# Entity batch times weights on one core: x and W packed side by side in memory, larger and smaller transfers, one reduce for the three parts

## What is computed

```python
def reference(r_entity_idxs, L0_rec_W):       # (1024, 12500) of 0.0 and 1.0, (128, 12500), float32
    entities = jnp.einsum('be,le->bl', entity_idxs, W)
    s = jnp.sum(entity_idxs, axis=1)
    s_safe = jnp.where(s != 0, s, 1.0)
    scale = jnp.where(s != 0, 1.0 / s_safe, 1.0)
    return entities * scale[:, None]          # (1024, 128)
```

## Time and profile before

| | |
|---|---|
| time, median of 3 runs | 155.78 us |
| span of the profiled execution (first to last instruction) | 154.0 us |
| TensorE busy | 133.4 us, 87% |
| VectorE, ScalarE busy | 90.6 us, 80.3 us |
| DMA | 58.20 MB, mean 378 GB/s |

### The profile page before, as it was taken

How to read it: one execution, slowest core, us unless ns; L and a number is a source line. 1 busy time by engine, 2 the same in 40 slices (tenths; PEclk the granted TensorE clock), 3 DMA queues, 4 the chain that set the end, 5 groups by cost and what they waited for, 6 DMA issues and landing times.

```text
span 154.0 us, 2291 instructions
## 1 busy us (share of the span) xinstructions
PE 133.4 (87%) x785; PEld 76.6 (50%) x785; DVE 90.6 (59%) x93; ACT 80.3 (52%) x103; POOL 0.5 (0%) x8
## 2 busy tenths in 40 slices
PE   0198999989989989989989989989989989999900
PEld 0043656545545545546545545545545545545500
DVE  0443975838538528628727826835845746648950
ACT  3462755464474464465456447437527527556720
POOL 1000000000000000000000000000000000000000
PEclk9999999999999999999999999999999999999985
DMA  5999999999999999999999999999999999999220
GB/s 165 320 417 423 412 429 421 412 422 419 421 421 417 422 422 417 426 419 419 421 421 419 421 419 418 424 417 419 426 417 413 432 417 406 349 348 346 90 61 4
DMA packets 13866, 58.20 MB, mean 378 GB/s; under 512 B 1148, under 2 KB 6480, under 8 KB 8228
## 3 DMA queue, kind: packets, MB, share of 16 engines
q1 hardware_dynamic: 13860, 58.13, 94.2%
HBM read 57.60 MB, written 0.52 MB: 377 GB/s over the span
## 4 chain that ended last, share of the span: by engine, by line
DMA 61%; PE 12%; issue 7%; DVE 6%; ACT 5%; SPq 4%; ACTq 0%; DVEq 0%
DMA x_sb<-x_t 61%; PE acc L414 12%; DVE w_parts L308 4%; ACT w_parts L230 3%; ACT act_out L236 1%; SPq L152 1%; SPq L156 1%; DVE w_rest L301 1%; ACT w_parts L224 1%; SPq L170 1%; SPq L190 0%; DVE y_sum L354 0%; SPq L161 0%; SPq L166 0%; DVE low_max L313 0%
## 5 line engine op out<-in xcount | busy, mean ns | idle before, releaser
L414 PE MATMUL acc<-w_parts,x_sb 128*128 128x385 bf16 (+1 forms) x784 | 133.2, 331 | 13.1 <-DVE w_parts L308 7.8
L414 PEld LDWEIGHTS acc<-w_parts,x_sb 128*128 128x128 bf16 (+1 forms) x784 | 76.6, 99 | 69.4 <-issue 16.1
L236 ACT ACTIVATE act_out<-x_sb 128x2048 bf16<-128x2048 uint16 (+4 forms) x31 | 48.0, 1549 | 42.5 <-DMA x_sb<-x_t 42.5
L313 DVE TENSOR_REDUCE low_max<-x_sb 128x2048 uint16 (+4 forms) x31 | 56.5, 1831 | 1.6 <-DMA x_sb<-x_t 1.6
L301 DVE TENSOR_TENSOR w_rest<-w_raw,w_parts 128x1024 f32<-128x1024 f32 (+2 forms) x14 | 15.2, 1091 | 37.8 <-ACT w_parts L224 37.8
L308 DVE TENSOR_TENSOR w_parts<-w_rest,w_parts 128x1024 bf16<-128x1024 f32 (+2 forms) x14 | 15.2, 1093 | 16.0 <-ACT w_parts L230 16.0
L224 ACT ACTIVATE w_parts<-w_raw 128x1024 bf16<-128x1024 bf16 (+2 forms) x14 | 13.3, 955 | 18.4 <-PE acc L414 12.7
L230 ACT ACTIVATE w_parts<-w_rest 128x1024 bf16<-128x1024 bf16 (+2 forms) x14 | 13.1, 943 | 1.9 <-DVE w_rest L301 1.9
L236 ACT ACTIVATION_READ_ACCUMULATOR act_out<-x_sb (+2 forms) x31 | 5.8, 187 | 0.0
L354 DVE TENSOR_TENSOR y_sum<-acc,y_sum 128x128 f32<-128x128 f32 x16 | 4.4, 280 | 0.8 <-ACT y_sum L269 0.7
L269 ACT ACTIVATE y_sum<-acc 128x128 f32<-128x128 f32 x8 | 2.2, 275 | 3.0 <-PE acc L414 2.9
(11 more groups left out here) (7 smaller groups left out, 0.8 us busy)
## 6 DMA issues: line engine op xcount, KB each, us to landing
x_sb<-x_t SPq DMA_DIRECT2D x46, 1024.0 KB, 16.5
w_raw<-w_t SPq DMA_DIRECT2D x12, 512.0 KB, 12.9
x_sb<-x_t SPq DMA_DIRECT2D x3, 512.0 KB, 9.4
x_sb<-x_t SPq DMA_DIRECT2D x4, 256.0 KB, 7.8
out<-y SPq DMA_DIRECT2D x4, 128.0 KB, 2.2
x_sb<-x_t SPq DMA_DIRECT2D x1, 336.0 KB
w_raw<-w_t SPq DMA_DIRECT2D x1, 64.0 KB
w_raw<-w_t SPq DMA_DIRECT2D x1, 42.0 KB
```

Source lines behind the costliest of these rows:

```text
L236: nc.scalar.activation(act_out[0:rows, buf, 0:tiles * n].rearrange("p (j b) -> p j b", j=tiles), low, ACT.Copy, accum_out=low_max[0:rows, ...
L313: nc.vector.tensor_reduce(low_max[0:rows, bass.ds(col, 1)], low, AX.XY, ALU.max).then_inc(dve_checked, count)
L414: return nc.tensor.matmul(acc[:, b, 0:N], x_top[0:rows, s, j, b * P:(b + 1) * P], w_parts[0:rows, s, j, :], start=first, stop=last)
```

## The change

x and W are laid out by the host in the order in which they are loaded. `main` holds 20 units; in a unit each of 128 partitions has one row of 18432 B: x of 4 tiles (4 x 4096 B) and W of 4 tiles (4 x 512 B) of the unit that follows. `ends` holds the pieces of both ends: a short one (84 rows, x and W of one tile), two ramp pieces (x of 1 and 2 tiles; W of 3 and 4), six taper pieces (x of 2, 2, 2, 2, 1, 1 tiles; the first two with W of 4 and 6 tiles), and the x of the last 4 tiles in six final pieces by users: three of 256 users x 4 tiles, one of 128 x 4, two of 128 x 2. 4 slots of one unit stand in place of 2 of a block; ramp, taper and final pieces have buffers of their own. SP waits, for a unit, until its slot's 32 matmuls and both checks are done.

`rest` and `lo` now read the upper halves of the words themselves and no longer wait for ScalarE's `hi` and `mid`. The three parts of a bank are added by one `tensor_reduce` from PSUM on VectorE, ScalarE does all the scaling, and the banks go out in pairs but for the last two, each alone. Users are dealt to banks in another order (`reshape(P, B // P, E)`), so that a pair of banks is written in rows of 1024 B. The general path works tile by tile in a loop; TensorE's part of it is 48 matmuls long in place of 272.

```diff
-T = 8
-CHUNK = 2
-CHUNKS = T // CHUNK
-SLOTS = 2
...
-PIECE = 2
+T = 4
+SLOTS = 4
+MAIN = 20
+RAMP_X = (1, 2)
+RAMP_W = (3, T)
+TAPER_X = (2, 2, 2, 2, 1, 1)
+TAPER_W = (T, 6, 0, 0, 0, 0)
+LAST = 4
+FINAL = ((0, 2, 0, 4), (2, 4, 0, 4), (4, 6, 0, 4), (6, 7, 0, 4), (7, 8, 0, 2), (7, 8, 2, 4))
+TILES = sum(RAMP_X) + MAIN * T + sum(TAPER_X)
...
+def pieces(short, B, L):
+    shapes = [(short, B + L)]
+    shapes += [(P, x * B + w * L) for x, w in zip(RAMP_X, RAMP_W)]
+    shapes += [(P, x * B + w * L) for x, w in zip(TAPER_X, TAPER_W)]
+    shapes += [(P, (j1 - j0) * (b1 - b0) * P) for b0, b1, j0, j1 in FINAL]
+    at, table = 0, []
+    for rows, cols in shapes:
+        table.append((at, rows, cols))
+        at += rows * cols
+    return table, at
...
-    LOADS = [(q, 0, T) for q in range(PIECES - 2)]
-    LOADS += [(PIECES - 2, j, j + T // 2) for j in range(0, T, T // 2)]
-    LOADS += [(PIECES - 1, j, j + CHUNK) for j in range(0, T, CHUNK)]
-    LAST_COL = BLOCKS * CHUNKS
-    CHECKS = LAST_COL + 2 * len(LOADS)
...
-        x_sb = sb("x_sb", [P, SLOTS, T, B], F32)
-        w_raw = sb("w_raw", [P, SLOTS, T, L], F32)
-        w_rest = sb("w_rest", [P, T, L], F32)
-        w_parts = sb("w_parts", [P, SLOTS, T, N], BF16)
-        low_max = sb("low_max", [P, CHECKS], F32)
-        act_out = sb("act_out", [P, 2, CHUNK * B], BF16)
+        ROW = T * (B + L)
+        xw = sb("xw", [P, SLOTS, ROW], F32)
+        xw_short = sb("xw_short", [P, B + L], F32)
+        xw_ramp = [sb(f"xw_ramp{k}", [P, x * B + w * L], F32) for k, (x, w) in enumerate(zip(RAMP_X, RAMP_W))]
+        xw_taper = [sb(f"xw_taper{k}", [P, x * B + w * L], F32) for k, (x, w) in enumerate(zip(TAPER_X, TAPER_W))]
+        x_final = [sb(f"x_final{k}", [P, (j1 - j0) * (b1 - b0) * P], F32) for k, (b0, b1, j0, j1) in enumerate(FINAL)]
+        w_rest = sb("w_rest", [P, 2, 6 * L], F32)
+        parts_short = sb("parts_short", [P, 1, N], BF16)
+        parts_ramp = sb("parts_ramp", [P, RAMP_W[0], N], BF16)
+        parts_main = sb("parts_main", [P, SLOTS, T, N], BF16)
+        parts_a = sb("parts_a", [P, TAPER_W[0], N], BF16)
+        parts_b = sb("parts_b", [P, TAPER_W[1], N], BF16)
+        low_max = sb("low_max", [P, 2 * CHECKS], F32)
...
+        def unit_count(u):
+            return u + 3
...
+        PAIRS = [(b, b + 2) for b in range(0, BANKS - 2, 2)] + [(BANKS - 2, BANKS - 1), (BANKS - 1, BANKS)]
...
-            def load_w(m, s):
-                sp.dma_start(w_raw[:, s, :, :].rearrange("p j l -> p (j l)"),
-                             w_blocks[m - 1].rearrange("p j l -> p (j l)")).then_inc(w_in[s], 16)
-            def load_x(m, s, c):
-                sp.dma_start(x_sb[:, s, chunk(c), :].rearrange("p j b -> p (j b)"),
-                             x_blocks[m - 1, :, chunk(c), :].rearrange("p j b -> p (j b)")).then_inc(x_in[s][c], 16)
-            def free_chunk(m, c):
-                sp.wait_ge(products_done, m * CHUNKS + c + 1)
-                sp.wait_ge(act_checked if c % 2 else dve_checked, m * CHUNKS + c + 1)
...
-            load_x_head(0)
-            for k, (row, rows) in enumerate(head):
-                sp.dma_start(w_raw[0:rows, 0, k, :], w_t[row:row + rows, :]).then_inc(w_head_in, 16)
-            load_x_head(1)
-            load_w(1, 1)
-            load_x(1, 1, 0)
-            load_x(1, 1, 1)
-            sp.wait_ge(split_done, 1)
-            load_w(2, 0)
-            load_x(1, 1, 2)
-            load_x(1, 1, 3)
-            with sp.Fori(1, BLOCKS // 2) as i:
...
+            def load_main(m, s):
+                sp.dma_start(xw[:, s, :], main[m]).then_inc(main_in[s], 16)
+            sp.dma_start(xw_short[0:short, :], piece(0)).then_inc(short_in, 16)
+            for k in range(NR):
+                sp.dma_start(xw_ramp[k][:, :], piece(1 + k)).then_inc(ramp_in[k], 16)
+            for s in range(SLOTS):
+                load_main(s, s)
+            with sp.Fori(1, MAIN // SLOTS) as i:
                 for s in range(SLOTS):
-                    m = 2 * i + s
-                    sp.wait_ge(split_done, m)
-                    load_w(m + 1, 1 - s)
-                    for c in range(CHUNKS):
-                        free_chunk(m - SLOTS, c)
-                        load_x(m, s, c)
-            for c in range(CHUNKS):
-                free_chunk(BLOCKS - SLOTS, c)
-            for k, (q, j, end) in enumerate(LOADS):
-                sp.dma_start(x_sb[:, 0, j:end, users(q)],
-                             x_blocks[BLOCKS - 1, :, j:end, users(q)]).then_inc(last_in[k], 16)
-            for q in range(PIECES):
-                sp.wait_ge(y_ready, (q + 1) * PIECE)
-                sp.dma_start(out[users(q), :].rearrange("(b p) l -> p b l", p=P),
-                             y[:, q * PIECE:(q + 1) * PIECE, :]).then_inc(y_out, 16)
+                    m = SLOTS * i + s
+                    sp.wait_ge(products_done, m - SLOTS + EDGE + 1)
+                    sp.wait_ge(dve_checked, m - SLOTS + EDGE + 1)
+                    sp.wait_ge(act_checked, m - SLOTS + EDGE + 1)
+                    load_main(m, s)
+            for k in range(NT):
+                sp.dma_start(xw_taper[k][:, :], piece(1 + NR + k)).then_inc(taper_in[k], 16)
+            for k in range(NF):
+                sp.dma_start(x_final[k][:, :], piece(1 + NR + NT + k)).then_inc(final_in[k], 16)
+            for b0, b1 in PAIRS:
+                sp.wait_ge(y_ready, b1)
+                sp.dma_start(out_pairs[:, b0:b1, :], y[:, b0:b1, :]).then_inc(y_out, 16)
...
+                def load_full(x, w):
+                    sp.dma_start(x_full, x).then_inc(full_in, 16)
+                    sp.dma_start(w_full[:, 0:L], w).then_inc(full_in, 16)
...
+                with sp.Fori(1, MAIN) as i:
+                    for j in range(T):
+                        sp.wait_ge(full_used, T * i + j + 1 + sum(RAMP_X))
+                        load_full(main[i, :, j * B:(j + 1) * B],
+                                  main[i - 1, :, T * B + j * L:T * B + (j + 1) * L])
...
-            def hi(s, shape=WHOLE):
-                for rows, tiles in shape:
-                    op = nc.scalar.activation(part(s, 0, rows, tiles), w_top[0:rows, s, tiles, :], ACT.Copy)
-                op.then_inc(hi_done, 1)
-            def mid(m, s, shape=WHOLE):
-                act.wait_ge(rest_done, m + 1)
-                for rows, tiles in shape:
-                    op = nc.scalar.activation(part(s, 1, rows, tiles), rest_top[0:rows, tiles, :], ACT.Copy)
-                op.then_inc(mid_done, 1)
...
-            def step(m, s, x_landed, w_landed):
-                act.wait_ge(w_in[1 - s], w_landed)
-                act.wait_ge(products_done, m * CHUNKS)
-                hi(1 - s)
-                check(m, s, 1, x_landed)
-                mid(m + 1, 1 - s)
-                check(m, s, 3, x_landed)
...
+            def split(words, parts, n, buf, count, rows=P):
+                nc.scalar.activation(parts[0:rows, 0:n, 0:L], top(words, n), ACT.Copy)
+                act.wait_ge(rest_done, count)
+                rest = top(w_rest[0:rows, buf, 0:n * L], n)
+                nc.scalar.activation(parts[0:rows, 0:n, L:2 * L], rest, ACT.Copy).then_inc(top_parts_done, 1)
+            def low_sum(words, n, col, buf, rows=P):
+                size = words.shape[1]
+                nc.scalar.activation(act_out[0:rows, buf, 0:size].rearrange("p (j f) -> p j f", j=n), low(words, n),
+                                     ACT.Copy, accum_out=low_max[0:rows, bass.ds(CHECKS + col, 1)]).then_inc(
+                                         act_checked, 1)
...
+            with act.Fori(0, MAIN // SLOTS) as i:
+                for s in range(SLOTS):
+                    m = SLOTS * i + s
+                    act.wait_ge(main_in[s], 16 * (i + 1))
+                    act.wait_ge(products_done, m + 1)
+                    split(main_w(s), parts_main[:, (s + 1) % SLOTS, :, :], T, (s + 1) % 2, unit_count(m + 1))
+                    act.wait_ge(act_checked, m + EDGE - 1)
+                    low_sum(main_x(s, T // 2, T), T // 2, m + EDGE, (s + 1) % 2)
...
+            def check_final(k):
+                size = x_final[k].shape[1]
+                c = EDGE + MAIN + NT + k
+                act.wait_ge(final_in[k], 16)
+                act.wait_ge(act_checked, c - 1)
+                low_sum(x_final[k][:, size // 2:size], 1, c, c % 2)
+            pair = 0
+            for k, (b0, b1, j0, j1) in enumerate(FINAL):
+                check_final(k)
+                if k and FINAL[k - 1][3] == LAST:
+                    for b in range(*FINAL[k - 1][0:2]):
+                        scale(b, pair)
+                    pair += 1
+            scale(BANKS - 1, pair)
...
-            def step(m, s, x_landed):
-                dve.wait_ge(split_done, m + 1)
-                rest(m + 1, 1 - s)
-                check(m, s, 0, x_landed)
-                lo(m + 1, 1 - s)
-                check(m, s, 2, x_landed)
...
+            def rest(words, n, buf, rows=P):
```

(141 more changed lines are left out.)

370 lines of the change are left out of this document (191 added, 179 removed).

## The result

151.07 us against 155.86 for the kernel before in the same comparison (median of 4 each): ratio 0.971, 95% interval 0.967 to 0.975. The forecast was 149.9 us, with a range of 148.2 to 153.4. The profiled execution's span is 149.4 us in place of 154.0; the sum had 148.1.

What follows compares the result with a forecast made beforehand. Transfers bound the middle, TensorE's slow untaken-path branch the end. Span 154.0 less 3.0 to the last matmul and 2.9 behind it gives 148.1; with 1.78 outside the span, 149.9 us, range 148.2 to 153.4.

Steps and rivals of the forecast that it cites:

- the sum: Whole span: 154.0 less 3.0 up to the last matmul and 2.9 behind it, 148.1 us.
- The packet's price: Loads: 9.4 ns plus 0.0368 ns per byte for a packet, so 5.50 us for a unit of 18432 B rows.
- The rival of long rows cut short: Main loads: long rows bring nothing or are cut at 8192 B; units of 5.61 to 5.65, time 152.5; chance 0.18.
- The last unit's landing: End of main's loads: lands at 119.5 us, bounds 118.9 and 120.7.
- the prediction's sum of packets: Loads up to the landing at 25.56 before: 21.4 us of packets, leaving 4.15 for first issue, slow start and receipt.
- rows 6: Profile rows of TensorE's instruction queue: 0.02 MB fetched at 26 to 28, 138 to 140 and 150 to 152 us.
- The last matmul: TensorE's tail: 144 matmuls, 23.8 us, after main's last landing; ends at 143.3 us against 146.3.
- Behind the last matmul: Kernel's end: reduce some 544 ns, VectorE done at 2.1 us, output landed at 4.5, end at 4.8 instead of 7.7.
- T: The time at which TensorE's last matmul ends, forecast at 143.3 us.
- The branch: TensorE's jump over the general path: 0.06 us in place of 3.78; rival that it still stalls, 153.0 us, chance 0.13.
- The clock: TensorE at the ramp: half clock after 2 us idle would cost 16 matmuls 2.6 us, won back over main; cost none.
- The term outside the span: Median of runs above the profiled span: 1.78 us, which the change doesn't touch.

Runs made afterwards that it cites:

- part 2: Changed kernel with each unit loaded by four transfers of 4608 B rows: 155.40 us; by two transfers, x and W apart: 152.60 us.
- Part 7: Changed kernel again, unedited: 151.18 us; with final checks first and main's last unit in two transfers: 149.87 us; last four units so: 149.96 us.
- part 4: Changed kernel with the checks of the six final pieces ahead of all finishing on VectorE and ScalarE: 150.42 us, 0.966.
- part 5: Changed kernel with ScalarE copying lo and VectorE adding twice: 154.90 us; with checks first and lo copied one pair ahead: 150.45 us.
- Part 1: Kernel before with TensorE's untaken general path cut to 32 matmuls: 152.67 us; changed kernel with 224 matmuls put back into it: 154.04 us.
- part 3: Changed kernel with TensorE's loop over main written out: 151.29 us, 0.973; beside it, trace packets sorted by inference into 16 DMA engine chains.

## Why the prediction was right, and what it missed

The forecast's 149.9 us was 1.2 under the measured 151.07. Its mechanisms held; one term is missing from its sum, the fetch near 24 us, with about 1.25 us. A start some 0.2 us quicker than summed and an end 0.2 us longer make up the rest; they cancel.

- **The packet's price** held: 5.50 us a unit forecast, 5.50 measured, and the runs of part 2 lie on the same line. The rival of long rows cut short is refuted by the count of packets and by those runs. The Trainium skill's 425 GB/s (DMA: Bandwidth & Descriptors, Bandwidth) is passed by this case's 429.
- **The last unit's landing** was forecast at 119.5 with bounds to 120.7 and came at 120.43. The first unit of main landed at 14.71, where the sum had 14.9, so start and packets were right; what was missing is the term for the instruction fetch. The step that was short is the prediction's sum of packets: it began from a landing at 25.56 us, just ahead of the fetch of before, and so saw nothing of it. The fetch itself was in rows 6, which were read for the branch alone.
- **The last matmul**: 23.8 us behind that landing were forecast, 23.94 measured; 144.37 in place of 143.3 is the fetch again. Part 7 shows why an earlier landing alone doesn't shorten it: TensorE is still at the unit ahead.
- **Behind the last matmul**: the reduce took 549 ns (544 forecast), VectorE was done at T + 2.35 (2.1), the output landed at T + 4.46 (4.5), the end was T + 5.0 (4.8). VectorE is late next, as said; part 4 shows it by experiment, and part 5 that the one reduce, which the prediction priced rightly, is worth nothing beside three additions in a good order.
- **The branch**: 0.35 us in place of 3.78, forecast 0.06; hidden under the output either way (the branch is over at 148.52, the output lands at 148.83). Part 1 shows that the path's length is the cause. The Trainium skill (Runtime: NRT & Kernel Launch, Instruction fetch mechanics) says that a taken branch out of the blocks at hand must fetch its target; the long and the short path agree, 3.74 and 0.21 us, but the fetches in the traces account for 0.9 to 1.4 us of the stall and not for all of it.
- **The clock** cost nothing: after an idle of 0.77 us at the ramp TensorE went on at 0.164 us a matmul, and after 2.27 us in the run of part 4 as well. So the half rate that the prediction allowed for after 2 us did not come.
- **The term outside the span**: 1.67 us between span and median, 1.78 before.

What stays open: that a fetch strikes one DMA engine, which one, and that it and not the start of the refilling makes the long gap, is read from our sorting alone. Why the first unit lands up to 1 us later in some executions is not known; it bears on whether the landings move by 0.4 or by 1.3 us at the fetch. And 2.4 us or more of the slow branch have no fetch beside them.

## What to carry to other kernels

Look at the last microseconds of every engine, the sequencers' rows included: a branch over a long path that is never run cost 3.0 us, and all the rest of this change gave 1.8. Price packets by two sizes found in the trace, and here three others could be foretold to 0.2%. In a stream that is bound by transfers, a small one that strikes a single DMA engine can move every later landing, so put it into the sum. When transfers and an engine run at nearly the same rate, ask where the engine stands at each landing, not when the data lands; and after each gain at the end ask who starts last, for the order that helped one step before may be the next bound.

## What the runs showed of the hardware

A fetch of TensorE's instructions (16 KB) goes through the DMA engines beside the data, and takes 1.1 us in the middle of the load. At the first one in the kernel after, all later landings moved by 1.25 us, by the reading of part 3. Over the runs of this case the same step was 0.4 to 1.3 us. Four more of them in the same stream moved the landings by little (one unit started 5.83 us after the one ahead, the others of that stretch 5.50), which the sorting in part 3 explains by one engine struck at a time.

And the first matmuls ran 0.32 us apart, twice 0.164, until about 11.6 us in the kernel after and 12.0 in the kernel before, while the granted clock of that stretch is given as 1.00 (the third figure from the end; 16 matmuls in 4.5 us):

```profile
6.50:11.00 4.50, 4.50 (x16) 2.10 (x15) 3.67 (x7) 3.59 (x9) 0.00 (x0) 1.00 1.04 440
```

What held them to half the rate is not shown.
